# A tokenised attention and expert tower on one core: the order of gathers, roots and products ahead of the attention loop

## The reference

```python
# 8 sequences of 1024 tokens, 128 channels
combined = concat([table_n[hash_n(bytes)] for n in (2, 3, 4)])   # 3 x 128 wide
h = combined @ proj_w.T + proj_b
x = layernorm(h)
x_down = conv1d(x, dw, stride=2, pad=1) + db                     # 512 positions
# three branches, each softmax(q k) v and a layernorm:
#   cross: q(x), k(x_down), v(x_down)
#   dot:   q(x), k(x), v(x)
#   cos:   q(x)/|q|, k(x)/|k|, v(x), logits divided by a temperature
h = h + gate-weighted sum of the three branches
h = h + experts(layernorm(h))        # 32 experts, each takes its 256 best tokens
```

## Time and profile before

| | us |
|---|---|
| median of 3 runs | 1281.1 (1280.67 to 1286.17) |
| span of the profiled execution | 1262.3 |
| the profiled execution's own time | not among the records; the median less the span is 18.8 |
| PE busy in the span | 1077.9 (85%) |
| DVE busy | 843.0 (67%) |
| POOL busy | 735.0 (58%) |
| ACT busy | 686.9 (54%) |

### The profile page before, as it was taken

One profiled execution on the slowest core, in us unless ns is written; L12 is line 12 of the kernel. 1 busy time (PEld: TensorE's weight loads), 2 busy tenths in 40 slices (PEclk: granted clock), 3 DMA queues, 4 the chain that ended last, 5 costly groups with the idle time before them and its releaser, 6 DMA issues. The chain is left out here.

```text
span 1262.3 us, 23453 instructions
## 1 busy us (share of the span) xinstructions
PE 1077.9 (85%) x7553; PEld 954.0 (76%) x7553; DVE 843.0 (67%) x2699; ACT 686.9 (54%) x1765; POOL 735.0 (58%) x1188
## 2 busy tenths in 40 slices
PE   4679999999999999999999999999992367767662
PEld 3569989988989989998998999898881145556451
DVE  5356777787777867877786787777775866654210
ACT  1446756666575666667566666756653544423220
POOL 6266684766467657746765774443442045677774
PEclk9879999999999999999999999999995567799786
DMA  3010000100001101100110110000002013344442
GB/s 106 15 36 22 22 24 28 30 25 18 20 26 32 33 10 43 31 10 26 32 33 9 44 30 10 12 9 20 12 19 68 0 39 60 67 74 90 76 69 21
DMA packets 49086, 42.64 MB, mean 34 GB/s; under 512 B 6728, under 2 KB 44488, under 8 KB 48840
## 3 DMA queue, kind: packets, MB, share of 16 engines
q0 software_dynamic: 18432, 22.04, 9.3%
q1 hardware_dynamic: 30536, 19.13, 5.0%
HBM read 27.51 MB, written 13.63 MB: 33 GB/s over the span
## 5 line engine op out<-in xcount | busy, mean ns | idle before, releaser
L637 PE MATMUL mixed<-v,pT 128*128 128x131 f32 x2560 | 318.4, 276 | 0.7 <-DVE o L883 0.7
L637 PEld LDWEIGHTS mixed<-v,pT 128*128 128x128 f32 x2560 | 301.6, 191 | 0.9 <-issue 0.8
L876 DVE TENSOR_REDUCE neg_max<-scores 128x1 f32<-128x1024 f32 (+1 forms) x192 | 199.1, 1037 | 49.4 <-PE scores L439 48.8
L1107 POOL DMA_INDIRECT gram<-in_emb,ids x192 | 192.5, 1002 | 62.2 <-issue 51.8
L1035 ACT ACTIVATE probs<-scores,neg_max 128x1024 f32<-128x1024 f32 (+1 forms) x192 | 186.6, 972 | 24.9 <-DVE neg_max L876 24.6
L1044 ACT ACTIVATE pT<-turned 128x512 f32<-128x512 f32 x211 | 125.3, 594 | 64.9 <-PE turned L618 64.4
L1158 POOL TENSOR_TENSOR zb<-row,gate 128x384 f32<-128x384 f32 x64 | 54.5, 852 | 142.9 <-DVE gate L911 142.5
L437 PE MATMUL scores<-k_hi,q_hi 128*128 128x512 f32 x320 | 135.5, 423 | 2.3 <-DVE q_lo L776 2.3
L1919 POOL DMA_INDIRECT out_h<-yw,slots x64 | 102.4, 1599 | 49.1 <-DVE yw L1768 22.4
L618 PE MATMUL turned<-con,probs 128*128 128x128 f32 x844 | 123.8, 276 | 6.6 <-ACT probs L1035 1.8
L439 PE MATMUL scores<-k_hi,q_lo 128*128 128x512 f32 x320 | 126.7, 396 | 0.0
(11 more groups left out here) (306 smaller groups left out, 2445.6 us busy)
## 6 DMA issues: line engine op xcount, KB each, us to landing
wd<-in_w_down SPq DMA_DIRECT2D x32, 171.0 KB
token_table<-w SPq DMA_DIRECT2D x16, 320.0 KB, 2.4
out_h<-h SPq DMA_DIRECT2D x16, 256.0 KB, 2.3
gram<-in_emb,ids POOLq DMA_INDIRECT x192, 2.6
wu<-in_w_up SPq DMA_DIRECT2D x8, 170.5 KB, 4.2
w<-in_weights SPq DMA_DIRECT2D x1, 1174.0 KB, 7.8
xg<-token_table,slots POOLq DMA_INDIRECT x64, 2.7
out_h<-yw,slots POOLq DMA_INDIRECT x64
```

The costliest lines, as they stand in the source:

```text
L637: last = pe.matmul(mixed[:, 0:C + 3], pT[:, n % 2, j * P:(j + 1) * P], vals[:, 0:C + 3], start=(j == 0), stop=(last_half and j == half * 4 ...
L876: dve.tensor_reduce(neg_max[:, n % 4:n % 4 + 1], scores[:, (n % 2) * S:(n % 2) * S + width], AX_X, ALU.max, negate=True).then_inc(maxed, 1)
L1107: pool.indirect_dma_start(gram[:, t % 4, g, :], None, emb[g], bass.IndirectOffsetOnAxis(ap=ids[:, s, t, g:g + 1], axis=0)).then_inc(gather ...
```

## The change

```diff
-AHEAD_OF_LOOP = """gram0 gram1 gram2 gram3 gram4 gram5 xT0 k_d0 gram6 q_d0 q_cr0 gram7 v_dc0 gram8 qk_raw0 qk_raw1 v_dc1 v_dc2 v_dc3
-    xT1 down0 k_d1 k_cr0 qk_raw2 qk_raw3 v_cr0 v_cr1"""
+AHEAD_OF_LOOP = """gram0 gram1 gram2 gram3 gram4 gram5 gram6 gram7 xT0 gram8 k_d0 qk_raw0 qk_raw1 q_d0 q_cr0 v_dc0 v_dc1 v_dc2 v_dc3
+    xT1 qk_raw2 qk_raw3 down0 k_d1 k_cr0 v_cr0 v_cr1"""
@@ scalar, ahead of the loop
-                if ITEMS[k] == ("gram", 0, 5):
+                if ITEMS[k] == ("gram", 0, 7):
                     normalise(0, 0)
                 if ITEMS[k] == ("qk_raw", 0, 1):
                     norm_squares(0, 0)
@@ gpsimd, ahead of the loop
             for t in range(2, NT):
                 gathers(0, t)
-                if t == 5:
-                    token_rstd(0, 0)
+            token_rstd(0, 0)
             token_rstd(0, 1)
-            cos_norm(0)
             for s in (2, 3):
                 for k in items_at(s):
                     if ITEMS[k][0] == "gram":
                         gathers(*ITEMS[k][1:])
+            cos_norm(0)
```

## The result

Over 20 runs each on one chip the changed kernel takes 1278.07 us (1274.82 to 1284.48), the kernel before 1282.78 (1280.55 to 1290.42): ratio 0.9967 [0.9951, 0.9983]. I had forecast 1281.6, half a microsecond slower than before. It is faster by 0.2 to 0.5%: a small gain, still within the 0.5% that I had called no change, but on the other side of my forecast, and clear of no change by its interval. The changed kernel's twenty times fall into two groups of ten, 1274.8 to 1276.9 with a mean granted clock of 0.931 to 0.934 and 1279.3 to 1284.5 with 0.925 to 0.929, so that its median stands in the gap between them; the profiled execution belongs to the first. It has a span of 1273.6 us and a time of its own of 1275.4: 1.8 us lie around the span.

The account below looks back on a forecast made before the run. TensorE bounds the loop, a chain of handovers the stretch before it; the chain's shifts end 0.5 us later at unit 3, so span 1262.3 becomes 1262.8, plus 18.8 from span to median gives 1281.6 us; range 1278.0 to 1285.5.

Parts of the forecast that it names:

- Step 1: First half: six more gathers go ahead of the first root; xT0 at 44.0 against 37.90, 6.1 us later.
- Step 2: Second root 2 us earlier, at 47.8, but unused: squares of qk_raw0 hold the second normalise, 0.15 us later.
- Step 3: ACT empties q_d0 and q_cr0 only after the second normalise, holding xT1: 56.8 against 53.58, 3.2 us later.
- rival C: xT1 isn't held, both halves come close together: sum of -2.7 us, 1278.4; chance 0.08.
- Step 5: Cosine root ready 3 us earlier, six gathers ahead of it hidden; cos_scale at 72.4, 1.7 us later.
- Step 4: qk_raw2 and qk_raw3 ahead of down and the convolution: unit 0's scores at 70.05 against 65.16, 4.9 us later.
- Step 6: To the loop's full speed: unit 2 1.0 us later with the clock slow there, unit 3 opens 0.5 us later.
- rival A: Faster: TensorE's clock doesn't fall before unit 2; -1.4 us, or -2.3 with the convolution fast, 1279; chance 0.17.

Follow-up runs that it names:

- e2: The changed kernel, unchanged, on the first chip, the one without unnamed waits: 1264.56 us, 0.9998 of the kernel before.
- e5: The changed kernel with ACT's second normalise moved directly behind k_d0 and the first squares behind q_cr0: 1275.88 us, 0.9918 of the kernel before.
- e1: The kernel before, unchanged, on the first chip, the one without unnamed waits: 1264.40 us.
- e11: The changed kernel with the cosine root again ahead of the six gathers of sequence 1: 1285.56 us, 0.9990 of the kernel before.
- e6: The kernel before, unchanged, on a chip with unnamed waits: 1285.43 us.
- e9: The kernel before with only the cosine root moved behind the six gathers of sequence 1: 1277.92 us, 0.9921 of the kernel before.
- e7: The changed kernel, unchanged, on a chip with unnamed waits: 1276.50 us, 0.9931 of the kernel before.
- e10: The kernel before with qk_raw2 and qk_raw3 ahead of down and the six gathers ahead of the cosine root: 1273.79 us, 0.9893 of the kernel before.
- e3: The kernel before with only qk_raw2 and qk_raw3 moved ahead of down, first chip: 1260.81 us, 0.9980 of the kernel before.
- e4: The changed kernel with qk_raw2 and qk_raw3 back behind down, k_d1 and k_cr, first chip: 1267.18 us, 1.0028 of the kernel before.
- e12: The changed kernel with qk_raw2 and qk_raw3 back behind k_cr, on a chip where before takes over 1280: 1283.99 us, 0.9974 of the kernel before.
- e13: The kernel before with two GpSimd waits put into its row of 15 gathers: 1288.15 us, 1.0050 of the kernel before.
- e8: The kernel before with only qk_raw2 and qk_raw3 ahead of down, on a chip with unnamed waits: 1277.93 us, 0.9947 of the kernel before.

## Why the prediction was wrong

**What was right.** On the chip without the waits the steps can be held against e2. Step 1: `xT0` 44.08 (I said 44.0). Step 2: second root 47.64 (47.8), second `normalise` 51.83 (51.95). Step 3: `q_hi` 53.37 (53.65), `xT1` 56.11 (56.8); e5 shows that ACT's order holds it, so rival C falls, though the 1278.4 that it gave is near the measured time. Step 5: DVE comes to `cos_scale` at 71.08 (72.4) without a wait for GpSimd, whose root is done by 66.7: the wait has moved as described. There the whole, no change, came out as well (0.9998), but by luck: the loop ended 3.3 us earlier, not 0.5 later, and the experts' stage of e2 took 5.4 us more than e1's, which no step of mine speaks of.

**What was off in size.** Step 3 gave `xT1` the slow clock; the turning took 0.60 us (I said 1.09), since the clock fell only at 56.93. Step 4 came out at 68.80 instead of 70.05. Step 6 let the clock be low at unit 2; it was 1.00 from 63.75 on, and unit 3 opened at 83.31 (83.09 by its first weight load, which rows 10 go by), not 87: rival A, which I had given 0.17, and more than the 1.4 to 2.3 us that I had for it. The prediction fell by its own bound here ("if unit 3 opens outside 84 to 91"). I had put the low clock at unit 2 down to the wait of 2.30 us right ahead of it. The rows have the fall at 71.92, within the wait of 3.52 us ahead of `k_c0` that ended at 72.70, and this wait is the one that the new order takes away; the longest between unit 1 and unit 2 is 1.94 us in e2. The Trainium skill ("TensorE: Matmul & The Clock Gate", "HAM oscillation — how this bites in real kernels"), which I had used for step 3, tells of waits between batches after which the next batch starts slow. The rows agree with it at the wait of 3.52 us. At the 1.94 us ahead of unit 2 they don't decide: in e2 no fall followed, in e11 the clock fell at 86.51 behind a wait of 1.94 us that ended at 86.34.

**The step that failed** is step 5, the six gathers: "hidden; without that cover they would cost 7.5". I asked only what the gathers delay, and not what is beside them where they were. On the chips where before takes over 1280 us they stood in front of nine others at the start of the loop, and DVE, ACT and then TensorE stood still there, which cost some 7.5 us (e6 against e1: 4.6 us later at unit 3, 12.1 at unit 4). The change takes them away. In return its row of 24 gathers in the first stretch adds ACT's second unnamed wait (5.76 us, of which about 2.6 reach unit 0: it is 75.95 - 68.80 = 7.15 us behind e2, where unit 0 of e9 and e6 is 4.5 to 4.6 behind e1's 65.62). At the end of the loop: e7 952.39 against e6 958.31, 5.9 us earlier; 3.3 of that are there without waits too (e2 against e1), so 2.6 are the waits, if the rest adds up as there. The two profiled executions differ by 8.5 us in all; the other 2.6 lie in the experts' stage (325.5 against 328.1 us) where the granted clock was at 0.50 for 167 and 177 us. How much of the first comparison's 4.7 us is of the one or the other kind isn't known: it has no profile of before with the waits.

**The sign that I explained away.** The median stood 18.8 us over the span, and I added this as a constant. In every run that has both, spans and times differ by 1.8. So 17 us of the timed runs were in no row that I read, and no estimate of mine could hold them. Nothing in the profile said where they were, but it could have been said that they were missing, and the range and the chances been made wider for it.

**What stays open.** Why TensorE's signals come late, and why only on some chips. They come late at rows of many gathers, at the same instructions from kernel to kernel in the loop, and in the first comparison and on three of the four chips of the experiments; that much the traces show. The Trainium skill ("Runtime: NRT & Kernel Launch", "Instruction fetch mechanics") says that each engine fetches its instructions in blocks by a DMA queue of its own and calls the cost "mostly hidden". I had thought of a fetch that stands behind the gathers' transfers. The traces speak against it: they list the instruction transfers (queues q8 and q14, 62 and 56 packets), and, ACT's first wait of each kernel aside, in 159 of the 163 unnamed waits none of them starts; around e6's long wait one starts at 86.20 and the next at 106.77. What they do show is that the gathers' landings leave fewer events on the chips with such waits (3522 to 3716 of all DMAs in a trace, against 6119 to 6127 without), so something in the signalling differs; no run shows what. e9 and e10 were not run on the chip where before takes 1264 us, so whether their gain is there as well (e10's would be at least e3's 0.2% if the gathers' move costs nothing) isn't known. The low clock in the experts' stage and the two groups of the changed kernel's times are without a cause that I could name.

## What to carry to other kernels

Compare the profiled execution's span with the timed median before anything else: it was 1.8 us less where both were of one execution, and a difference of 18.8 meant that the profile lacked 17 us of the timed runs; a forecast from such a profile has to say so. When the clock is low at a unit, look for the wait within which it fell, not for the last wait ahead of the unit. A row of transfers that delays nobody in its own queue may still stop other engines; when a change moves one, price the place that it leaves as well as the place that it goes to, and test it alone. A bundle of edits is best taken apart: here one edit of three, the products first, gained 0.2 to 0.5%, one line, the gathers ahead of the cosine root, 0.3 to 0.8% on the chips with unnamed waits, and the third, the bulk of the change, cost 0.3% (e4) to 0.5% (e12 against e9). And when an edit is to make a row shorter, count the row in its trace (e13).

## What the runs showed of the hardware

- The same kernel took 1263.7 us on one chip, and 1282.5, 1285.6 and 1287.6 on others (17 to 35 runs each). The profiles of the others have waits of DVE, ACT and GpSimd for signals of TensorE that come 1.5 to 7.4 us behind the recorded end of their products; on the first chip there were none in four profiles.
- Where they occur, each profile has them at about 23 to 25 us, while the first twelve gathers run (DVE 3.3 to 4.8 us, GpSimd 2.1 to 2.4; unit 0 is 4.6 us later in e6 than in e1 and 3.5 us in e8 than in e3), and seven or eight of 1.5 to 2.5 us on DVE in the loop, at its rows of six gathers, 13 to 16 us in sum. The loop (unit 3 to the last unit's scores) is 858 to 862 us long with them instead of 852, and 867 to 868 where a long wait comes behind unit 3 (e6, e11, e13).
- The second half of 24 gathers in the first stretch adds one of 4.3 to 5.9 us on ACT; 15 gathers at the start of the loop (in e8 12 and 3, with a pause) add one of 6.5 to 8.0 us on DVE, with up to 7.2 on ACT (e6, e8, e11).
- TensorE's granted clock in one kernel differs from execution to execution: 1.00 through unit 2 in three profiles of the changed kernel, 0.50 from 87.3 to 90.7 in the fourth (e7).
- The experts' stage goes with that clock: 323.5 to 327.3 us with 160 to 169 us at 0.50, 326.3 to 331.6 us with 172 to 180.
